# Flamingo block with gated experts: latents and media come in turned, their means and factors spread through DRAM

## The reference, cut to what matters

```python
ln  = layernorm(layernorm(x), gamma_lat, beta_lat)       # latents, 256 rows a sequence
xn  = layernorm(ctx_1024, gamma_media, beta_media)       # media, 256 rows a sequence
q   = (ln @ Wq + bq) * DH ** -0.5
k,v = split(concat([xn, ln]) @ Wkv + bkv)                # 512 keys, 8 heads of 128
x   = x + tanh(g_xattn) * (softmax(q @ k.T) @ v @ Wo + bo)
x   = x + tanh(g_ffn) * experts(layernorm(x))            # top 2 of 8 experts, 256 -> 1024 -> 256
```

## Time and profile before

| | before |
|---|---|
| median of 3 runs | 1544.16 us (1540.41 to 1545.47) |
| the profiled execution's time | 1537.72 us |
| its span | 1536.0 us |
| TensorE busy | 1499.6 us, 98% |
| weight loads of TensorE | 1381.2 us, 90% |
| VectorE busy | 1112.4 us, 72% |
| ScalarE busy | 950.0 us, 62% |
| GpSimd busy | 601.7 us, 39% |
| DMA in the attention stage | 8 to 35 GB/s |
| mean granted clock of TensorE | 0.996 |

### The profile page before, as it was taken

One profiled execution on the slowest core, in us unless ns is written; L12 is line 12 of the kernel. 1 busy time (PEld: TensorE's weight loads), 2 busy tenths in 40 slices (PEclk: granted clock), 3 DMA queues, 4 the chain that ended last, 5 costly groups with the idle time before them and its releaser, 6 DMA issues. The chain is left out here.

```text
span 1536.0 us, 29968 instructions
## 1 busy us (share of the span) xinstructions
PE 1499.6 (98%) x10446; PEld 1381.2 (90%) x10446; DVE 1112.4 (72%) x2689; ACT 950.0 (62%) x2057; POOL 601.7 (39%) x714
## 2 busy tenths in 40 slices
PE   8999999999999999999999999999889999999997
PEld 6889898898988888898888989888889999999996
DVE  7677777777777777777777777687796666666685
ACT  5555656556565555555565555655787777777775
POOL 5323424333342433434233342233455444444443
PEclk9999999999999999999999999999999999999999
DMA  4000100000000010000000000012855555445563
GB/s 158 10 22 8 22 8 22 28 1 29 8 22 8 22 29 8 22 8 22 8 22 28 8 22 8 8 27 85 227 126 132 129 147 141 129 126 151 136 173 83
DMA packets 57823, 91.13 MB, mean 59 GB/s; under 512 B 8617, under 2 KB 44774, under 8 KB 57550
## 3 DMA queue, kind: packets, MB, share of 16 engines
q1 hardware_dynamic: 41710, 70.19, 14.2%
q0 software_dynamic: 15824, 18.98, 7.0%
q10 hardware_dynamic: 144, 0.05, 0.0%
HBM read 70.91 MB, written 18.29 MB: 58 GB/s over the span
## 5 line engine op out<-in xcount | busy, mean ns | idle before, releaser
L885 POOL TENSOR_SCALAR probs<-probs,rsum 128x512 f32<-128x512 f32 x256 | 174.1, 692 | 532.4 <-DVE rsum L1559 532.2
L1091 ACT ACTIVATE pt_hi<-turn 128x512 fp32r<-128x512 f32 x256 | 139.1, 595 | 238.2 <-PE turn L1239 236.8
L910 POOL DMA_INDIRECT out_rows<-yo,token x71 | 121.6, 1713 | 206.7 <-DMA out_rows<-yo,token 134.5
L1676 DVE TENSOR_TENSOR ht_lo<-hs,ht_hi 128x512 fp32r<-128x512 f32 x142 | 98.2, 691 | 118.1 <-ACT ht_hi L1058 113.3
L1553 DVE TENSOR_REDUCE smax<-score 128x1 f32<-128x512 f32 x256 | 169.6, 684 | 13.1 <-PE score L189 12.7
L992 ACT ACTIVATE probs<-score,nbias 128x512 f32<-128x512 f32 x256 | 173.0, 685 | 3.9 <-DVE nbias L1555 3.8
L1049 ACT ACTIVATE hs<-ph,vecs 128x256 f32<-128x256 f32 (+1 forms) x284 | 114.1, 457 | 93.5 <-PE ph L189 82.4
L1786 DVE TENSOR_TENSOR pt_lo<-turn,pt_hi 128x512 fp32r<-128x512 f32 x256 | 164.1, 682 | 8.3 <-ACT pt_hi L1091 8.1
L187 PE MATMUL py<-w_hi,ht_lo 128*128 (+1 forms) x568 | 162.7, 286 | 3.2 <-DVE ht_lo L1676 3.2
L189 PE MATMUL py<-w_hi,ht_hi 128*128 (+1 forms) x568 | 160.6, 283 | 0.0
L188 PE MATMUL py<-w_lo,ht_hi 128*128 (+1 forms) x568 | 160.5, 283 | 0.0
(11 more groups left out here) (245 smaller groups left out, 4703.2 us busy)
## 6 DMA issues: line engine op xcount, KB each, us to landing
w_raw<-in_L_ffn_W SPq DMA_DIRECT2D x45, 1024.0 KB, 15.6
xhat_rows<-rows SPq DMA_DIRECT2D x16, 264.0 KB, 2.2
x_raw<-in_x SPq DMA_DIRECT2D x16, 256.0 KB, 3.2
c_raw<-in_ctx SPq DMA_DIRECT2D x16, 256.0 KB, 3.3
out_rows<-x SPq DMA_DIRECT2D x16, 256.0 KB, 2.5
xg<-xhat_rows,token POOLq DMA_INDIRECT x71, 4.5
out_rows<-yo,token POOLq DMA_INDIRECT x71
v_raw<-in_L_xattn_Wkv SPq DMA_DIRECT2D x2, 512.0 KB, 8.0
```

Source lines behind the costliest of these rows:

```text
L885: last = pool.tensor_scalar(probs[n % 2][:, t, :], probs[n % 2][:, t, :], rsum[:, n % 2, t:t + 1], 1.0, ALU.mult, ALU.mult)
L910: pool.indirect_dma_start(out=A["out"], out_offset=bass.IndirectOffsetOnAxis(ap=token[:, u:u + 1].bitcast(U32), axis=0), in_=yo_of(t)[:, s ...
L1091: act.activation(pt[0][:, 2 * t:2 * t + 2, :], turn[t][:, :].rearrange("p (j i) -> p j i", j=2), ACT.Copy).then_inc(s_pthi, 1)
```

## The change

The host hands over x and ctx a second time with rows along the free dimension (`x_turned`, `ctx_turned`, features first). SyncE loads them into a tile `zin` (the names of this text: turned rows). The means and factors of the 512 rows, which GpSimd makes as before but with rows on the partitions, go to a DRAM tensor in four DMAs of 4-byte elements, and come back in one DMA that gives every partition all 1024 values (`spread`, 512 KB written). VectorE adds the negated means and multiplies with the factors, in four instructions of 128x512 for each sequence: adding for quarter pair k = 0 in step 5, multiplying in step 6, adding for k = 1 in step 7 and multiplying in step 0, each behind the read of "k" and ahead of the read of "q". ScalarE then scales and shifts from SBUF at the end of step 0 (`scale_turned`). The "z" units of TensorE are gone, and so are the four normalising instructions of GpSimd. For sequence 1 the four VectorE instructions are in steps 2 and 3 of the loop's first sequence, and its split moves from step 2 to step 4. The planned order of units in the ring of banks is shorter by two in step 2. `load_w1(0)` now waits with `load_w2` for the last split.

```diff
-        if h == Z_STEP and b + 1 < B:
-            units += [("z", (b + 1, k)) for k in range(KD)]
...
+            spread=nc.dram_tensor("mean_and_factor", (B, 2, KEYS), F32, kind="Internal").ap(),
...
+            def load_turned(c):
+                if c == 1:
+                    sp.wait_ge(s_full, KD)
+                else:
+                    sp.wait_ge(s_zt, c - 1)
+                for name, cols in (("x_turned", slice(T, KEYS)), ("ctx_turned", slice(0, T))):
+                    sp.dma_start(zin[:, :, cols], A[name][c].rearrange("(k p) t -> p k t", p=P)).then_inc(s_turned_in, 16)
+            def spread_norms(c):
+                sp.wait_ge(s_rsa, c)
+                sp.wait_ge(s_z, c + 1)
+                for tiles, cols in ((slice(0, TT), slice(T, KEYS)), (slice(TT, JT), slice(0, T))):
+                    with nc.allow_non_contiguous_dma(reason="a value of each row"):
+                        for r in range(2):
+                            sp.dma_start(dram["spread"][c, r, cols].rearrange("(j p) -> p j", p=P), norms[:, r, tiles])\
+                                .then_inc(s_norms_out, 16)
+                sp.wait_ge(s_norms_out, 64 * c)
+                if c == 1:
+                    weights_split(sp, "k1")
+                else:
+                    sp.wait_ge(s_zin, KD * (c - 1))
+                sp.dma_start(spread[:, :, :].rearrange("p r t -> p (r t)"),
+                             dram["spread"][c].rearrange("r t -> (r t)").partition_broadcast(P)).then_inc(s_spread, 16)
...
+            load_turned(1)
+            spread_norms(1)
             sp.wait_ge(s_routing, N_ROUTING)
...
             load(2)
+            load_turned(2)
+            spread_norms(2)
...
                     load(b + 3)
+                    load_turned(b + 3)
+                    spread_norms(b + 3)
                 sp.wait_ge(s_rows, b + 1)
...
-                pow_rstd("a", rs_a, 4, s_rsa)
-                negate(mv_a)
-                own.wait()
-                pool.wait_ge(s_rsa, c)
-                pool.wait_ge(s_full, number["z", (c - 1, KD - 1)] + 1)
-                for t in range(TT):
-                    norm(z[:, TT + t, :], x_raw[c % 3][:, t, :], mv_a, rs_a, t)
-                for t in range(TT):
-                    last = norm(z[:, t, :], c_raw[c % 2][:, t, :], mv_a, rs_a, TT + t)
-                last.then_inc(s_z, 1)
+                if c >= 2:
+                    pool.wait_ge(s_norms_out, 64 * (c - 1))
+                own.wait()
+                pool.tensor_tensor(norms[:, 1, :], ve["a"][:, 0:JT], minus_half[:, 0:JT], ALU.pow).then_inc(s_rsa, 1)
+                pool.tensor_scalar(norms[:, 0, :], mv_a[:, :, 0], -1.0, 0.0, ALU.mult, ALU.add).then_inc(s_z, 1)
...
+                if i == 4:
+                    split_kv(1)
-                if h == Z_STEP and b + 1 < B:
+                if h == Z_STEP and 1 <= b < B - 1:
                     split_kv(b + 1)
...
+            def scale_turned(c):
+                act.wait_ge(s_zin, KD * c)
+                act.wait_ge(s_kvt, c)
+                for k in range(KD):
                     for s in range(2):
-                        last = act.activation(zt[:, k, s * T:(s + 1) * T], src[:, s * T:(s + 1) * T], ACT.Identity,
+                        cols = slice(s * T, (s + 1) * T)
+                        last = act.activation(zt[:, k, cols], zin[:, k, cols], ACT.Identity,
                                               scale=gamma[:, s, k:k + 1], bias=beta[:, s, k:k + 1])
+                last.then_inc(s_zt, 1)
...
+                if i == 3:
+                    scale_turned(1)
+                if i % H == 0 and 1 <= i // H < B - 1:
+                    scale_turned(i // H + 1)
...
-                elif kind == "z":
-                    c, k = at
-                    pe.wait_ge(s_z, c + 1)
-                    for j in range(JT):
-                        last = pe.transpose(dst[:, j * P:(j + 1) * P], z[:, j, k * P:(k + 1) * P], ident[:, :])
...
+            def centre(c, k):
+                dve.wait_ge(s_turned_in, 32 * c)
+                dve.wait_ge(s_spread, 16 * c)
+                own.mark(dve.tensor_tensor(zin[:, k, :], zin[:, k, :], spread[:, 0, :], ALU.add))
+            def normalise_turned(c, k):
+                own.wait()
+                dve.tensor_tensor(zin[:, k, :], zin[:, k, :], spread[:, 1, :], ALU.mult).then_inc(s_zin, 1)
...
+                    if u[0] == "k":
+                        if i in (2, 3):
+                            centre(1, i - 2)
+                        if h == N_STEP and b + 2 < B:
+                            centre(b + 2, 0)
+                        if h == N_STEP + 1 and b + 2 < B:
+                            normalise_turned(b + 2, 0)
+                        if h == N_STEP + 2 and b + 2 < B:
+                            centre(b + 2, 1)
+                        if h == 0 and 1 <= b < B - 1:
+                            normalise_turned(b + 1, 1)
                 if i < STEPS:
                     reciprocal_sum(i)
+                if i in (2, 3):
+                    normalise_turned(1, i - 2)
```

More of the change, by code:

```diff
@@ L114 @@
 A_STEP = 3
+N_STEP = 5
 Z_STEP = 2
@@ L286, in build @@
             zt = alloc(first, "zt", [P, KD, KEYS])
-            z = alloc(first, "z", [P, JT, D])
+            with ExitStack() as rows_of_first:
+                z = alloc(rows_of_first, "z", [P, JT, D])
+            zin = alloc(first, "z_turned", [P, KD, KEYS])
             kvt0 = [alloc(first, f"kvt0_{s}", [P, KD, KEYS], F32R) for s in pair]
@@ L291, in build @@
             kvt1 = [alloc(first, f"kvt1_{s}", [P, KD, KEYS], F32R) for s in pair]
-            early = dict(zt=zt, z=z, wkv=wkv, wq=wq, kvt=[kvt0, kvt1])
+            early = dict(zt=zt, z=z, zin=zin, wkv=wkv, wq=wq, kvt=[kvt0, kvt1])
             step = dict(v_sb=[[alloc(first, f"v0_{s}", [P, JT, HALF], F32R) for s in pair]])
@@ L356, in late @@
             return sb(name, shape, dt)
-        wkv, wq, kvt, zt, z = (early[n] for n in ("wkv", "wq", "kvt", "zt", "z"))
+        wkv, wq, kvt, zt, z, zin = (early[n] for n in ("wkv", "wq", "kvt", "zt", "z", "zin"))
         raw, v_sb, pt, probs, kt, qt, ot, wo = (
@@ L427, in layer @@
         pad_ids = sb("pad_ids", [P, P])
-        raw.update(k1=sb("k1_raw", [P, KD, INNER - FIRST_W]), q1=sb("q1_raw", [P, KD, INNER - FIRST_W]),
-                   o0=sb("o0_raw", [P, H // 2, D]), o1=sb("o1_raw", [P, H // 2, D]))
+        norms = sb("norms", [P, 2, JT])
+        with ExitStack() as raws:
+            raw.update(k1=alloc(raws, "k1_raw", [P, KD, INNER - FIRST_W]),
+                       q1=alloc(raws, "q1_raw", [P, KD, INNER - FIRST_W]),
+                       o0=alloc(raws, "o0_raw", [P, H // 2, D]), o1=alloc(raws, "o1_raw", [P, H // 2, D]))
+        spread = sb("spread", [P, 2, KEYS])
         x2, rows = [x2_0, x2_1], [rows0, rows1]
@@ L505, in layer @@
         s_z = sem("z_ready")
+        s_turned_in, s_norms_out, s_spread = sem("turned_in"), sem("norms_out"), sem("spread_in")
+        s_zin, s_zt = sem("turned_normalised"), sem("zt_ready")
         s_kvt, s_xn = sem("kvt_ready"), sem("xn_rows")
@@ L999, in read_unit @@
                 act.wait_ge(s_full, n + 1)
-                if kind == "z":
-                    c, k = at
-                    if c:
-                        act.wait_ge(s_kvt, c)
+                act.activation(x2t[:, :, :], src[:, :].rearrange("p (k t) -> p k t", k=KD), ACT.Copy).then_inc(s_aread, 1)
+            def scale_turned(c):
+                act.wait_ge(s_zin, KD * c)
+                act.wait_ge(s_kvt, c)
+                for k in range(KD):
                     for s in range(2):
-                        last = act.activation(zt[:, k, s * T:(s + 1) * T], src[:, s * T:(s + 1) * T], ACT.Identity,
+                        cols = slice(s * T, (s + 1) * T)
+                        last = act.activation(zt[:, k, cols], zin[:, k, cols], ACT.Identity,
                                               scale=gamma[:, s, k:k + 1], bias=beta[:, s, k:k + 1])
-                else:
-                    last = act.activation(x2t[:, :, :], src[:, :].rearrange("p (k t) -> p k t", k=KD), ACT.Copy)
-                last.then_inc(s_aread, 1)
+                last.then_inc(s_zt, 1)
             def hi_x(t):
@@ L1384, in _ @@
                 for u in steps[i]:
-                    if u[0] in "ztgr":
+                    if u[0] in "tgr":
                         unit(*u)
@@ L1898 @@
     aps["vectors"] = nc.dram_tensor("in_vectors", (P, VECS), F32, kind="ExternalInput").ap()
+    for name, of in (("x_turned", "x"), ("ctx_turned", "ctx_1024")):
+        arrays["in_" + name] = np.ascontiguousarray(np.asarray(inputs[of]).transpose(0, 2, 1))
+        aps[name] = nc.dram_tensor("in_" + name, (B, D, T), F32, kind="ExternalInput").ap()
     aps["out"] = nc.dram_tensor("out_rows", (TOKENS + P, D), F32, kind="ExternalOutput").ap()
```

7 lines of the change are left out of this document (3 added, 4 removed).

## The result

The changed kernel takes 1574.94 us (median of 4, 1571.73 to 1580.06) against 1542.29 us for the kernel before on the same chips; the ratio is 1.0213, with a 95% interval of 1.0178 to 1.0249. I forecast 1530.1 us and gave 1 chance in 20 to slower.

A forecast was written before the change was run, and what follows sets the result against it. TensorE, busy 1499.6 of 1536.0 us, was taken as the bound. 12.0 us from sequences 2 to 15 plus 2.1 from the first made 14.1, so 1544.16 - 14.1 = 1530.1 us, range 1523.5 to 1536.0.

The forecast's parts named there:

- what SyncE gets: SyncE's chain from means and factors through DRAM to VectorE's step 5 addition: 7.8 us taken, ends 7.0 and 17.5, 3.4 early.
- the landing of the four stores: Time until SyncE's four DMAs of 4-byte elements land in DRAM: 2.2 us, taken from writes to the lists.
- the window of 11.2: Time from the factors at 587.50 to the end of VectorE's read of "k" in step 5: 11.2 us, not narrowed.
- the prediction's paragraph on read-modify-writes: Skill's rule on writes under 512 B would add a second round trip: 10.0 us, not 7.8, still inside the window.
- Rival A: Spread too late for VectorE's first addition, step 5 (step 2 or 5 in first sequence); 1600 us at upper end; chance 0.05.
- its place, its price rule and its point: At VectorE's first addition, a chain over 12.5 us costs time; from 13.5 us the kernel is slower.
- my own upper end, 17.5 us: SyncE's chain with issues of 1.25, landing 2.2 and spread 10.3 us; would cost 5.0 us in each of 14 sequences.
- What was removed from TensorE: Transposes of step 2 (0.79 us) and slower matmul behind (0.07): 0.86 us a sequence, 12.0 us over sequences 2 to 15.
- The first sequence: VectorE, late in steps 1 to 3, gets through earlier, so step 4 starts earlier: 2.1 us gained, bounds 0 and 2.2.
- What VectorE and ScalarE got: Four VectorE instructions of 0.69 us in 0.95 us gaps, ScalarE's four moved to step 0's end; no steady-state cost.
- The rival of time given back in part (B): Step 3's reads or an added instruction come late, TensorE waits 0.56 us a sequence, 7.8 in all; 1538 us; chance 0.09.
- That the expert stage would swallow the gain (C): Expert stage waits for weight loads whose start doesn't move, so time stays at 1544 us; chance 0.04.

The follow-up runs named there:

- kernel with one store: The changed kernel with means and factors stored in one DMA of 32 bytes per partition, VectorE reading at a 32-byte stride; 1528.28 us, ratio 0.9910.

## Why the prediction was wrong, point by point

**The step that failed** is one term of the chain under "what SyncE gets": the landing of the four stores. I took 2.2 us for it, from the list DMAs. It was 7.3 us behind the last issue, 7.9 in the mean.

The 2.2 us was misread. The row "2.1/2.2/4.3" counts every DMA that touches the lists and has a landing, and the DMA view of the kernel before shows which these are:

```profile
expert_lists<-ids,place POOLq DMA_INDIRECT x64
...
early_names<-expert_lists SPq DMA_DIRECT2D x1, 3.0 KB, 2.1
early_names<-expert_lists SPq DMA_DIRECT2D x1, 2.0 KB, 2.2
names<-expert_lists,row POOLq DMA_INDIRECT x1, 4.3
```

All three landings are loads from the lists; none of the 64 stores of single values has one. What the trace does tell of those stores spoke against 2.2 us. SyncE waits for those of the first 14 sequences and then loads `early_names`. Here is first its wait, then the timelines of the last store and of the load:

```profile
SPq L732 <- DMA expert_lists<-ids,place: 19.3, 1, 19.3
```

```profile
1021.90 0.96 POOL L862 DMA_INDIRECT expert_lists<-ids,place  x1 [0.30 <-issue]
...
1030.80 1.58 SPq L737 DMA_DIRECT2D early_names<-expert_lists  x2
```

That is 8.9 us from the last store's issue to the load, with about 1 us of SyncE's own between its wait and the load. The stores there are GpSimd's indirect ones, one behind another, so this is no clean price; but with some 8 us for the landing my sum would have been 1.6 + 8 + 4 = 13.6 us, past the window of 11.2 and at the point where the kernel gets slower. The same 2.2 us carried the prediction's paragraph on read-modify-writes, which therefore had no ground in this trace. And I did not look at where the bytes go: the experiments show that the same four stores, spaced, land early enough.

The other terms came out close: 2.3 us for the issues (I had 1.6), 0.3 for the spread's issue, 4.5 for its landing (I had 4 with the issue in it). The chain from the first issue to the addition was 14.9 us in the sequence shown, against a window of 11.2. The window was right: from the first issue at 609.01 to the end of the read of "k" at 620.06 there are 11.05 us.

**Rival A** was what happened, with its place, its price rule and its point. Its rule was chain less 12.5 us for each sequence; 14.9 - 12.5 = 2.4, and step 5 grew by 2.4. That sequence is one of the dearer ones: over all 15 waits TensorE stood for 30.7 us, 2.0 each. Less the 13.2 us of gain (below) that gives some 17 over before. Measured: 32.7 in the medians, 34.6 in the profiled loop. The difference is what the rule did not have: the granted clock at 1.2 GHz around six of the waits, some 12 us in all, and the 5 us in other steps. I gave the case 0.05 though my own upper end, 17.5 us, was beyond its point of 13.5, and the middle of my ends was 12.25. With no like row in the trace, "near the lower end" was not an argument; the emptiness of the DMA engines says nothing on how long a store takes to be confirmed.

**What was removed from TensorE** came out as worked out. The kernel with one store shows 0.79 us less in step 2 and 0.11 less in step 3, and 65.6 us for a sequence in place of 66.43, 0.80 us against my 0.86; steps 5, 6, 7, 0 and 1 are about 0.02 us longer each. 14 x 0.80 = 11.2 us. The first sequence gave 69.70 - 67.70 = 2.0, where I had 2.1. Together 13.2 against my 14.1, and 14.7 between the medians.

**What VectorE and ScalarE got** was free, as forecast: four instructions of 0.68 to 0.69 us in gaps of 0.95. Even 1.17 us each was. ScalarE's scaling at the end of step 0 took 0.03 us from TensorE at most (step 1 lasts 7.90 to 7.93 us). The rival of time given back in part (B), which had 0.56 us a sequence, is not seen in any kernel in which the spread was in time, but for these hundredths and the single long steps. That the expert stage would swallow the gain (C) isn't seen either.

**The first sequence** had the spread late twice. For sequence 1 VectorE waited 4.85 us in step 2, which then lasted 13.26 us in place of 10.60; I had taken it to be 2.2 us early there, by the same wrong term. For sequence 2 step 5 lasted 11.63 us in place of 7.90.

## What to carry to other kernels

Before a landing in a profile is taken as a price, see whether it is that of a store or of a load, and which DMA it belongs to. Price a store by where its pieces land, not only by their size: single elements from 128 partitions, side by side in DRAM, were confirmed after 7.5 us, and 32 bytes from each partition after 1.4 to 1.9. Let each partition write what it has in one piece, and do the reordering on the reading side, where it cost half a microsecond of an engine that had it to spare. When a round trip through DRAM must end at a fixed place, compare its upper bound with the window; if the bound is outside and the next step is as good a place, take the later one: that alone was worth 37 us.

## What the runs showed of the hardware that I had not expected

A store's landing grew with the number of separate pieces within a few hundred bytes of DRAM: 1.9 us for up to 16 pieces in 512 bytes, 2.7 to 3.4 for 32, 3.2 to 4.7 for 64, 7.5 for 128, while in 11 of 15 sequences of the changed kernel the last packet of the four stores had been sent 0.8 us behind the last issue.

VectorE's tensor_tensor of 128x512 in fp32 with one operand read at a stride of 32 bytes took 1.17 us in place of 0.69. In step 0 it then stretched GpSimd's list DMA beside it, which the contiguous form had left at 0.96 us:

```profile
613.01 0.96 POOL L894 DMA_INDIRECT expert_lists<-ids,place  x1 [0.31 <-issue]
614.28 1.47 POOL L894 DMA_INDIRECT expert_lists<-ids,place  x1 [0.30 <-issue]
```

The Trainium skill ("SBUF — State Buffer", Who interferes with whom) says that a VectorE instruction with two SBUF inputs contends with GpSimd's reads; these two rows of the kernel with one store agree, with 0.5 us: the second starts while VectorE's strided instruction (613.71 to 614.90) runs. And some waits of TensorE cost more than their length: behind one of 2.2 us the granted clock was at 1.2 GHz for 3.4 us, another 1.5 us lost. This was so at six of the 15 waits.
